# Transposes of the v projection issued one chunk later, behind the next chunk's matmuls

## What is computed

```python
# branch 1, "ret": retention, 16 heads of 128
q, k, v = jnp.split(x @ w_qkv, 3, axis=-1)
q = _xpos(q); k = _xpos(k)                 # rotary with decay
scores = einsum('bhtd,bhsd->bhts', q, k) * D ** -0.5 * mask
y = einsum('bhts,bhsd->bhtd', scores, v)
out1 = (silu(x @ w_g) * groupnorm(y)) @ w_proj
# branch 2, "ffn": a transformer layer, 16 heads of 128, F = 8192,
# routed per token against two cheap alternatives
scores = where(causal, q @ k.T / sqrt(128), -1e9)
ctx = softmax(scores) @ v
x2 = x + ctx @ wo.T
out2 = x2 + gelu(layer_norm(x2) @ w_ff1.T) @ w_ff2.T
result = x0 + out1 * silu(routed(out2))
```

## Time and profile before

| what | us |
|---|---|
| time, median of 2 runs | 5993.24 (5967.52 to 6018.95) |
| the profiled execution, its own time | 5757.14 |
| its span, slowest core | 5755.6 |
| spans of the 8 cores | 5736.3 to 5755.6 |
| matmuls (PE), busy | 3800.4, 66% |
| VectorE (DVE), busy | 1634.7, 28% |
| ScalarE (ACT), busy | 902.1, 16% |
| GpSimd (POOL), busy | 372.4, 6% |

### The profile page before, as it was taken

The page is one execution under the profiler, slowest core; times in us unless marked ns, Lnnn a source line. Parts: engine busy times, 40 slices in busy tenths (PEclk is TensorE's granted clock), DMA queues, the critical chain, the costliest instruction groups (busy, mean ns, idle before and its releaser), DMA issues.

```text
span 5755.6 us, 63523 instructions; the slowest of 8 cores (5736.3 to 5755.6 us)
## 1 busy us (share of the span) xinstructions
PE 3800.4 (66%) x18468; PEld 1743.5 (30%) x18468; DVE 1634.7 (28%) x3980; ACT 902.1 (16%) x1869; POOL 372.4 (6%) x330
## 2 busy tenths in 40 slices
PE   1277676767676677556566656656647399969496
PEld 1123333333333222223233223323322144423232
DVE  5713323232323214732222222222221400012222
ACT  2101111111111132011221222122210011100000
POOL 0000000000000000100000000000000011111010
PEclk9998888888888888777667766776769699989798
DMA  3214222222222234705434533543514244466665
GB/s 105 73 16 52 34 39 34 39 34 39 34 39 26 30 50 57 90 10 63 59 43 52 70 48 45 65 61 43 77 40 56 57 107 110 113 164 149 176 152 136
DMA packets 396792, 386.32 MB, mean 67 GB/s; under 512 B 309152, under 2 KB 333984, under 8 KB 389312
## 3 DMA queue, kind: packets, MB, share of 16 engines
q0 software_dynamic: 336960, 268.72, 33.4%
q1 hardware_dynamic: 59520, 113.54, 6.0%
HBM read 508.31 MB, written 109.05 MB: 107 GB/s over the span
## 4 chain that ended last, share of the span: by engine, by line
PE 54%; DVE 19%; issue 9%; DMA 9%; ACT 7%; DVEq 1%; ACTq 0%; SPq 0%; POOLq 0%; POOL 0%
PE pbA L842 5%; PE pbB L842 5%; PE pbB L1814 4%; PE pbB L783 4%; DMA wff<-ff2T_bf 4%; PE pbA L783 4%; PE pbA L1674 3%; PE pbB L1674 3%; ACT scp L1013 3%; PE pbA L724 3%; PE pbS L1094 2%; DVE scT_sb L1072 2%; PE pbA L988 2%; PE pbY L1094 2%; PE pbB L724 2%
## 5 line engine op out<-in xcount | busy, mean ns | idle before, releaser
L842 PE MATMUL pbA<-xn_allT,wvh 128*128 128x512 bf16 x1024 | 294.0, 452 | 36.7 <-DVE vtok L868 13.6
L842 PE MATMUL pbB<-xn_allT,wvh 128*128 128x512 bf16 x1024 | 259.9, 412 | 52.2 <-DVE vtok L868 39.8
L1814 PE MATMUL pbA<-xn_allT,wff 128*128 128x512 bf16 x1024 | 227.3, 383 | 94.9 <-DMA xn_allT<-hg_sp 80.7
L1674 PE MATMUL pbA<-bufA,wqh 128*128 128x512 bf16 x1024 | 234.2, 382 | 76.0 <-DVE bufA L1637 68.2
L1094 PE MATMUL pbY<-vtok,scT_sb 128*128 128x128 bf16 x1024 | 111.6, 273 | 228.9 <-DVE scT_sb L1075 120.8
L868 DVE COPY vtok<-pbT 128x512 bf16<-128x512 bf16 x128 | 54.4, 425 | 724.0 <-PE pbT L860 724.0
L1060 PE MATMUL pbT<-eye_sb,scp 128*128 128x128 bf16 x2304 | 251.3, 279 | 2.1 <-DVE scp L1003 0.2
L1814 PE MATMUL pbB<-xn_allT,wff 128*128 128x512 bf16 x1024 | 232.7, 390 | 25.8 <-DMA wff<-ff2T_bf 25.8
L1094 PE MATMUL pbS<-vtok,scT_sb 128*128 128x128 bf16 x1280 | 134.6, 271 | 171.6 <-DVE scT_sb L1075 111.1
L783 PE MATMUL pbB<-xn_allT,wkh 128*128 128x512 bf16 x1024 | 233.1, 381 | 2.0 <-DVE kb_sb L799 2.0
L783 PE MATMUL pbA<-xn_allT,wkh 128*128 128x512 bf16 x1024 | 231.4, 379 | 1.1 <-PE pbD L754 0.2
(11 more groups left out here) (287 smaller groups left out, 5238.2 us busy)
## 6 DMA issues: line engine op xcount, KB each, us to landing
wff<-ff2T_bf POOLq DMA_DIRECT2D x32, 2048.0 KB, 15.3
ff1T_bf<-ff1T POOLq DMA_DIRECT2D x8, 4096.0 KB, 42.5
ff2T_bf<-ff2T POOLq DMA_DIRECT2D x8, 4096.0 KB, 39.2
wqh<-ff1T_bf POOLq DMA_DIRECT2D x64, 512.0 KB, 5.8
p0x<-x_all SPq DMA_DIRECT2D x16, 1024.0 KB, 4.8
xn_allT<-hg_sp SPq DMA_DIRECT2D x2, 8192.0 KB, 39.3
p0x<-x_own SPq DMA_DIRECT2D x8, 1024.0 KB, 4.9
wqh<-w_qkv POOLq DMA_DIRECT2D x16, 512.0 KB, 7.4
```

The costliest lines, as they stand in the source:

```text
L842: inst = t.matmul(pb[key][:, 0:cw], self.wv_h[buf][:, ct, :], self.xn_allT[:, ct, c0:c0 + cw], start=(ct == 0), stop=(ct == CT - 1))
L1674: inst = t.matmul(pb[key][:, 0:cw], self.wq_h[buf][:, ct, :], self.bufA[:, ct, c0:c0 + cw], start=(ct == 0), stop=(ct == CT - 1))
L1814: inst = t.matmul(pb[key][:, 0:cw], wff2[buf][:, ft, :], hg3[:, ft, 0:cw], start=(ft == 0), stop=(ft == FT - 1))
```

## The change

In the V loop, the transposes of a chunk and the copy of their result into `vtok` are no longer appended right behind the chunk's eviction. They are kept in a closure and appended one iteration later, just behind the next chunk's 16 matmuls and ahead of the next chunk's eviction. Those of the fourth chunk are appended behind the loop. The order on TensorE goes from M0 T0 M1 T1 M2 T2 M3 T3 to M0 M1 T0 M2 T1 M3 T2 T3 (M: 16 matmuls, T: 4 transposes). The instructions and their number are the same. The eviction of chunk i still waits for the `vtok` copy of chunk i-1, which now stands behind chunk i's matmuls.

```diff
--- before.py
+++ after.py
@@ -832,6 +832,29 @@
                 k_src, k_done = self.kb_sb, list(k_ev)
 
             vg = []
+            tp_defer = [None]
+
+            def _v_tp(c0, cw, tkey, ev, vt):
+                def go():
+                    def _(t, c0=c0, cw=cw, tkey=tkey, ev=ev, vt=vt):
+                        self.wt(t, ev, *self.bfree[tkey])
+                        for k in range(cw // P):
+                            inst = t.transpose(pb[tkey][:, k * P:(k + 1) * P],
+                                               vt[:, k * P:(k + 1) * P],
+                                               self.eye_sb[:])
+                        self.inc(inst, s_t)
+                    self.T(_)
+                    tg2 = self.tok(s_t)
+
+                    def _(v, c0=c0, cw=cw, tkey=tkey, tg2=tg2):
+                        self.wt(v, tg2)
+                        self.inc(v.tensor_copy(self.vtok[:, c0:c0 + cw],
+                                               pb[tkey][:, 0:cw]), s_v)
+                    self.V(_)
+                    self.bfree[tkey] = [self.tok(s_v)]
+                    return [self.tok(s_v)]
+                return go
+
             for ci, (c0, cw) in enumerate(cfg.all_chunks):
                 key = "A" if ci % 2 == 0 else "B"
                 vt = self.vtmp if ci % 2 == 0 else self.vtmp2
@@ -845,6 +868,8 @@
                     self.inc(inst, s_t)
                 self.T(_)
                 tg = self.tok(s_t)
+                if tp_defer[0] is not None:
+                    vg = tp_defer[0]()
 
                 def _(s, cw=cw, key=key, tg=tg, vt=vt, vgl=list(vg)):
                     self.wt(s, tg, *vgl)
@@ -853,23 +878,8 @@
                 ev = self.tok(s_s)
                 self.bfree[key] = [ev]
                 tkey = "T" if ci % 2 == 0 else "T2"
-
-                def _(t, c0=c0, cw=cw, tkey=tkey, ev=ev, vt=vt):
-                    self.wt(t, ev, *self.bfree[tkey])
-                    for k in range(cw // P):
-                        inst = t.transpose(pb[tkey][:, k * P:(k + 1) * P],
-                                           vt[:, k * P:(k + 1) * P], self.eye_sb[:])
-                    self.inc(inst, s_t)
-                self.T(_)
-                tg2 = self.tok(s_t)
-
-                def _(v, c0=c0, cw=cw, tkey=tkey, tg2=tg2):
-                    self.wt(v, tg2)
-                    self.inc(v.tensor_copy(self.vtok[:, c0:c0 + cw],
-                                           pb[tkey][:, 0:cw]), s_v)
-                self.V(_)
-                self.bfree[tkey] = [self.tok(s_v)]
-                vg = [self.tok(s_v)]
+                tp_defer[0] = _v_tp(c0, cw, tkey, ev, vt)
+            vg = tp_defer[0]()
             v_done = self.tok(s_v)
             self.g_v = []
```

## The result

| | before | changed |
|---|---|---|
| time, median of all runs | 5895.73 (10 runs) | 5533.74 (11 runs) |
| ratio to the kernel before | 1 | 0.959, interval 0.956 to 0.962 |
| profiled execution, span | 5755.6 | 5518.9 |

The changed kernel is 4.1% faster. Run again beside the last two experiments it gave 0.961 (0.959 to 0.964). The profiled execution has a span 236.7 us shorter; the forecast for it was 232.7. In six of the ten runs before and four of the eleven after, some cores had a lower clock and the time was some per cent longer; the ratio leaves those out, and so it is not that of the two medians (0.939).

The account below looks back on a forecast made before the run. TensorE was taken to set the pace, its matmuls busy 66% of the span. 174.3 us from reordering V plus 58.4 from the clock made 232.7, giving 5760 us from a 5993.24 median, range 5495 to 5845.

Parts of the forecast that it names:

- The second gap as waiting instructions: In V, between transposes and next matmuls: time of eight long-satisfied waits, 0.80 us in ret, 0.91 in ffn.
- Chunk to chunk: Between V's matmul groups: 3.45 us for the first step, 3.80 for the next two, each 5.86 before.
- The last chunk: End of V: T2, copy, eviction and T3 in series, 5.42 us after the last matmuls start, a loss of 0.80.
- The sum without the clock: V over all 32 heads: the reordering alone gains 174.3 us.
- The clock: V's matmul groups stay at the upper clock level except ret's chunk 0, which keeps 31.0 us: gain 58.4 us.
- What follows V: From T3 to the next head: duration depends on the state V leaves, about 25 us either way in all.
- The third rival: Behind V: gain given back in the mixed-clock scores, about 25 us either way; chance 0.06 shared with both other rivals together.
- The time itself: Whole kernel: 232.7 us off the two timed runs' median of 5993.24, giving 5760.5 us, 3.9% less.

Follow-up runs that it names:

- the last two experiments: Changed kernel with evictions waiting for the copy two chunks before, 0.955; that kernel with ffn sums of squares spread over K and V, 0.920; both to the kernel before.
- the one with the waits once: Kernel before, with the eight g_v waits ahead of V's chunk 0 only: 0.974 of the kernel before; the same edit on the changed kernel gave 0.956.
- the one with 32 waits: Changed kernel with the eight g_v waits ahead of V's chunks 1 to 3 written four times: 0.973 of the kernel before.
- the same step on the sums of squares: Loosened-eviction kernel, with ffn squares, column sums and row scaling spread over K and V, only the row's transposes behind T3: 0.920 of the kernel before.
- the waits written twice: Kernel before, with the eight g_v waits ahead of V's chunks 1 to 3 written twice: 1.007 of the kernel before.
- the free eviction: Changed kernel, with a chunk's eviction waiting for the vtok copy of two chunks before instead of the last one: 0.955 of the kernel before.

## Why the prediction was right

*The second gap as waiting instructions.* Right, and shown: taken away, doubled, quadrupled, it goes, doubles, and comes back in the changed kernel. It is the step on which most hung, since the trace named another releaser. One detail was wrong: the first ffn head is not without such waits. `g_v` is set to one token behind the projections (L1346), and that head has gaps of 0.17 to 0.34 us ahead of its chunks 1 to 3.

*Chunk to chunk.* 3.45 us as forecast for the first; 3.68 instead of 3.80 for the others. The 0.35 us for the transposes was read where they stood behind a wait. With matmuls ahead of them they add 0.23. That is 32 x 2 x 0.12 = 8 us too little gain.

*The last chunk.* 5.31 us for 5.42. The hand-over from the copy to ScalarE was taken at 0.20 and is 0.10, the lower bound: 3 us.

*The sum without the clock.* 174.3 forecast. V gained 249.6, of which the clock has 58.8, so 190.8. 11 of the 16.5 us between are the two steps just named. Some 4 more come from taking one head for all: without slow groups V took 22.36 us in the mean of 15 ffn heads of the kernel before, where I had 22.20, and the first ffn head, with its one wait, took 20.25 for 19.44. So the 236.7 us of the profiled execution lie nearer to the forecast of 232.7 than the working deserves: V gave 17 us more than forecast, and 13 us came back outside V, which the prediction did not have.

*The clock.* 58.4 forecast. The time of V's groups behind chunk 0 above 3.615 us fell from 58.9 to 0.1. Ret's chunk 0 keeps its excess, 31.6 us in 16 heads where I had 31.0. That the clock follows the gaps is borne out by three kernels: the changed one, the one with the waits once, and the one with 32 waits have no slow group in 96, on any of the eight cores; with a round trip of 1.0 us and a second gap of 0.9 or 1.8 us close behind it there are 35 and 27. What exactly makes a group fall stays open: gaps of up to 1.2 us ahead of groups did not do it in the kernel with 32 waits, nor did gaps of 1.0 us ahead of the transposes in the one with the waits once.

*What follows V.* The third rival's bounds held for the mean: 38.8 us from T3 to the next ret head, 66.1 for ffn, against 38.4 and 66.1. Nothing was given back there.

*The time itself.* 5760 was forecast and 5533.74 measured, in the lower part of the range. It lies inside only because the range had been made wide enough to hold executions as quick as the profiled one. The difference, 3.9%, was right (0.959); the level was not. I took it off the median of two runs, 5993.24. Ten runs of the same kernel have a median of 5895.73, and the profiled execution, at 5757.14, was the better guide: less 232.7 it gives 5524.4.

## What to carry to other kernels

On an engine that works in order, put the consumer of a round trip over other engines behind the next independent block, and look at every wait instruction too, even those long satisfied. Behind a wait that blocks they cost 0.1 us each on TensorE's path; behind matmuls in flight they are free until the cover is used up. A short gap that appears exactly where a list of tokens is long, and is missing where the list is empty, is such a list, whatever releaser the profile names. When a deferral has worked once, look for the next serial chain behind it: the same step on the sums of squares gave 203 us more.

## What the runs showed of the hardware that was not expected

*A clock between the two levels.* In the profiles of the experiments, some heads of the ret stage ran with V groups of 4.37 us, neither 3.62 nor 5.3. From M1 to T0 it is 4.20 us, 262 ns a matmul, for 3.45. The window over three such groups, in the changed kernel with the waits once, shows a granted clock of 0.81 (the figure ahead of the last two):

```profile
724.30:737.30 13.00, 12.91 (x56) 5.70 (x56) 0.85 (x2) 1.79 (x3) 0.00 (x0) 0.81 0.00 0
```

```profile
724.25 4.38 PE L865 MATMUL pbB<-xn_allT,wvh 128*128 128x512 bf16 x16
728.45 0.44 PE L842 MATMUL pbT<-eye_sb,vtmp 128*128 128x128 bf16 x4
728.71 4.37 PE L865 MATMUL pbA<-xn_allT,wvh 128*128 128x512 bf16 x15
```

On the slowest core it came in 6 to 24 of the 96 V groups behind chunk 0 in six of the seven profiles, with gaps in V and without. In the seventh, that of the waits written twice, K's groups show it (eight of 4.4 us on the slowest core). In neither profile of the first comparison does any core have it. It is the 17 us named above.

It falls on pairs of cores. In all seven profiles cores 0 and 1, 2 and 3, 4 and 5, or 6 and 7 have it in the same stretch, to within some 20 us, and the two other cores of the die don't. With the waits once in the kernel before, for instance, cores 4 and 5 have it between 701 and 1049 us of their spans and no other core at any time. With the free eviction, cores 4 and 5 have it in the ret stage, from 516 to 1260 us, and cores 6 and 7 only in the ff2 stage, from 4871 us on. Over the ret stretch the granted clock was 0.71 on cores 4 and 5 and 0.83 on cores 6 and 7. Core 4, then core 6:

```profile
520.00:1260.00 740.00, 548.31 (x2747) 263.29 (x2792) 254.76 (x596) 98.51 (x175) 42.48 (x54) 0.71 0.29 37
520.00:1260.00 740.00, 544.31 (x2984) 264.42 (x2982) 268.73 (x625) 104.31 (x185) 48.17 (x61) 0.83 0.31 41
```

The Trainium skill describes a level like it ("TensorE: Matmul & The Clock Gate", Part 1, the peak-current limiter: 13/16 of the clock, 0.8125, on the whole die, held while the load lasts). The size agrees. That the whole die falls, and that it stays down under load, does not agree with these traces, so whether it is the same limiter isn't shown. Either way it did not take the gain: the changed kernel has 0.961 where its slowest core had such stretches.

*Slow groups are not a matter of gap length alone.* Doubling the second gap to 1.8 us gave fewer slow groups than the gap of 0.9 us: 12 to 27 of 96 over the eight cores (27 on the slowest, some of them mixed with the level just described), against 32 to 37. That is one profile of each kernel.
